# A long-convolution kernel on one core: odd-block chunk sums as three split products, and the chunk sums issued behind half of the Toeplitz products

## The chip, the core and the metric

The kernel runs on one core of a Trainium2 chip. The metric is device time in microseconds (us) of one execution; lower is better. Five engines with their own in-order instruction streams take part: PE (matrix products), ACT, DVE and POOL (elementwise work) and SP (which here only starts DMAs). They meet through semaphores alone.

## The reference, cut to what matters

```python
P = dtA[:, :, None] * jnp.arange(length)            # H=128 channels, N=64 states, L=2048
K = 2.0 * jnp.einsum('hn,hnl->hl', Cs, jnp.exp(P)).real
u_m = x * mask                                       # 64 sequences x 128 channels x 2048
y = irfft(rfft(u_m, 4096) * rfft(K, 4096))[..., :2048]   # a causal convolution per channel
return x + (y + u_m * D[:, None]) * mask
```

All data are float32. Each channel has its own convolution kernel K, built from 64 complex exponentials.

## The kernel before, in words

The kernel computes the convolution without a transform. A sequence of 2048 is cut in 8 chunks of 256, and each chunk in an even and an odd block of 128. Inside a chunk the convolution is a Toeplitz product; between chunks 64 complex states (128 rows) carry the past. After a prologue that builds tables, one **slot** per channel runs 128 times: slots of the first 6 channels and of the last 8 are written out, the 114 between are a hardware loop over groups of 6 channels (`groups`, L215 to L224, with register channel numbers).

A product in float32 costs the PE several passes. Where precision allows, an operand is split into a rounded high part (type fp32r, written by ACT as a copy) and a low part (operand minus high part, written by DVE or POOL), and `three` (L828) issues three fp32r products: high times high, high times low, low times high.

In slot h the PE works for three channels: `here` = h, `one` = h+1, `two` = h+2. Its order before: `chunk_sums(one)`, which forms the new state contributions of the 8 chunks in PSUM bank `v` (three split products for the even blocks, L844, one float32 product for the odd blocks, L847); `turn_x(two)`, 8 transposes of x to PSUM banks `xt_even` and `xt_odd`; `toep_even/toep_odd(here)` for two of the four 128-column pieces; `turn_e(two)`, two transposes; the other two Toeplitz pieces; `from_state(here)`, 12 split products that add the states' part to `y`.

Between `chunk_sums` and `from_state` of a channel stands a scan over its 8 chunks, which goes to and fro between ACT and DVE on bank `v`. Its steps for channel h+1, with the names used below:

1. `turn_odds(h+1)` on ACT (two 64-row copies, in the trace `room<-v 64x192`), after the chunk sums.
2. `pairs(h+1)` on DVE (two dependent operations, `mid` and `v`, 128x192).
3. `turn_pairs(h+1)` on ACT (two copies, 64x128).
4. `fours(h+1)` on DVE (four operations, each dependent on the one before, 128x128 and 128x64). The last one releases `s_evens`; its end is called **E(h+1)** below.
5. `turn_evens(h+1)` on ACT (two copies, 64x192), at the head of ACT's next slot.
6. `odds(h+1)` on DVE (two dependent operations, 128x192), behind `choose(h)`, the two COPY_PREDICATED that merge the finished channel h.
7. `z_high(h+1)` on ACT and then `z_low(h+1)` on DVE: the split states, which `from_state(h+1)` reads.

Order of the other engines in slot h, before. ACT: turn_evens(h), f_high(h+1), turn_odds(h+1), t_high(h+1), z_high(h), x_high(h+2), e_high and e_odd(h+2), turn_pairs(h+1), x_odd(h+2). DVE: choose(h-1), odds(h), pairs(h+1), z_low(h), x_low(h+2), e_low(h+2), fours(h+1). POOL: two broadcast multiplications `tw1`, `tw2` (L421, L422) and their difference `pf` (L428), with `f_low` (L404) and `t_low` (L409) between and behind. SP: load_x(h+3), then, once the PE is through with the Toeplitz products of h, load_t(h+2), then store(h-1).

Of the kernel before, what the change touches and what calls it, by code (L numbers as in the profile page):

```python
# [48 lines left out]
def s4d_kernel(nc, x, length, log_dt, C, log_A_real, A_imag, D, out):  # L49
    ctx = ExitStack()  # L50
    with ctx:
# [52 lines left out]
        zhi = [sb(f"zhi{i}", [P, NC * B], F32R) for i in range(2)]  # L104
        zlo = [sb(f"zlo{i}", [P, NC * B], F32R) for i in range(2)]

        ehi = [sb(f"ehi{i}", [P, P], F32R) for i in range(2)]
        elo = [sb(f"elo{i}", [P, P], F32R) for i in range(2)]
        eod = [sb(f"eod{i}", [P, P]) for i in range(2)]

        tw1, tw2 = (room[:, i].rearrange("p (a b c) -> p a b c", a=2, b=SQ) for i in (5, 6))
        pf = [sb("pf0", [P, 2, CHUNK]), room[:, 7].rearrange("p (a q) -> p a q", a=2)]
# [88 lines left out]
        s_zlo = sem("s_zlo")  # L201
        s_ehi = sem("s_ehi")
        s_elo = sem("s_elo")
        s_eod = sem("s_eod")
        s_fhi = sem("s_fhi")
        s_flo = sem("s_flo")
        s_thi = sem("s_thi")
# [138 lines left out]
        @block.gpsimd  # L346
        def _(pool):
            done = [0]

            def link(ins):  # L350
                done[0] += 1
                ins.then_inc(s_gp, 1)
                pool.wait_ge(s_gp, done[0])


            link(pool.memset(zpad[:], 0.0))
            link(pool.memset(ident[:], 0.0))
            link(pool.affine_select(out=ident[:], in_=ident[:], compare_op=ALU.not_equal, fill=1.0, base=0,
                                    pattern=[[-1, P]], channel_multiplier=1))
            link(pool.iota(mask[0:B, :], pattern=[[2 * CHUNK, CPH], [1, CHUNK]], base=0, channel_multiplier=0))  # L360
            link(pool.iota(mask[B:P, :], pattern=[[2 * CHUNK, CPH], [1, CHUNK]], base=CHUNK, channel_multiplier=0))
            pool.engine_nop().then_inc(s_pool0, 1)


            pool.wait_ge(s_ex0, 1)
            pool.wait_ge(s_ca, 16 * 2)
            c_re = cin[:].rearrange("p (n c) -> p c n", c=2)[:, 0, :]
            c_im = cin[:].rearrange("p (n c) -> p c n", c=2)[:, 1, :]
            pool.tensor_tensor(t1, ar, ar, ALU.mult)
            link(pool.tensor_tensor(t2, ai, ai, ALU.mult))  # L370
            pool.tensor_tensor(norm, t1, t2, ALU.add).then_inc(s_norm, 1)
            link(pool.tensor_tensor(t3, c_im, ai, ALU.mult))
            link(pool.tensor_tensor(g_re, c_re, ar, ALU.mult))
            link(pool.tensor_tensor(g_re, t3, g_re, ALU.subtract))
            link(pool.tensor_tensor(t3, c_im, ar, ALU.mult))
            link(pool.tensor_tensor(g_im, c_re, ai, ALU.mult))
            link(pool.tensor_tensor(g_im, g_im, t3, ALU.add))
            pool.wait_ge(s_norm, 2)
            pool.tensor_tensor(g_re, g_re, norm, ALU.mult).then_inc(s_g, 1)
            pool.tensor_tensor(g_im, g_im, norm, ALU.mult).then_inc(s_g, 1)  # L380

            pool.memset(NB[:, SQ - 1, 1, :], 1.0)
            link(pool.memset(NB[:, SQ - 1, 2, :], 0.0))
            pool.wait_ge(s_lam, 1)
            room_x = W1[:, 0].rearrange("p h i -> p (h i)")
            temps = [room_x[:, q * SQ // 2 * N:(q + 1) * SQ // 2 * N] for q in range(4)]
            link(level(pool, link, NB, 1, 2, 0, temps, 0))
            link(level(pool, link, NB, 1, 2, 0, temps, 1))
            level(pool, link, NB, 1, 2, 0, temps, 2).then_inc(s_nb, 1)
            pool.wait_ge(s_nb, 1)  # L390
            level(pool, link, NB, 1, 2, 0, temps, 3).then_inc(s_nb, 1)

            pool.wait_ge(s_nx, 1)
            part = SQ // 2 * (N - XSPLIT)
            temps = [wide[:, a:a + part] for a in (0, part, 2 * npn, 2 * npn + part)]
            level(pool, link, NX, 0, 1, A_POW, temps, 3, XSPLIT, N).then_inc(s_nxp, 1)
            for t in range(T_R - BANKS, T_R):
                pool.wait_ge(s_free[t % BANKS], t // BANKS + 1)

            def f_low(g, j):  # L400
                pool.wait_ge(s_fhi, chan(g, j) + 1)
                if exists(g, j, -2):
                    pool.wait_ge(s_y, 2 * chan(g, j) - 2)
                pool.tensor_tensor(flo[j % 2][:], pf[j % 2][:, 1, ::-1], fhi[j % 2][:].bitcast(F32),  # L404
                                   ALU.subtract).then_inc(s_flo, 1)

            def t_low(g, j):
                pool.wait_ge(s_thi, chan(g, j) + 1)
                pool.tensor_tensor(tlo[j % 2][:], traw[j % 2][:, ::-1], thi[j % 2][:].bitcast(F32),  # L409
                                   ALU.subtract).then_inc(s_tlo, 1)  # L410

            def channel(g, j):

                h, k = chan(g, j), j % 2
                w1 = W1[:, :, h].unsqueeze(3).broadcast_to([P, 2, SQ, SQ])
                w2 = W2[:, :, h].unsqueeze(3).broadcast_to([P, 2, SQ, SQ])
                b1 = B1[:, h].unsqueeze(1).unsqueeze(1).broadcast_to([P, 2, SQ, SQ])
                b2 = B2[:, h].unsqueeze(1).unsqueeze(1).broadcast_to([P, 2, SQ, SQ])
                if exists(g, j, -1):
                    pool.wait_ge(s_pf, h)  # L420
                pool.tensor_tensor(tw1[:], w1, b1, ALU.mult).then_inc(s_gpa, 1)  # L421
                pool.tensor_tensor(tw2[:], w2, b2, ALU.mult).then_inc(s_gpa, 1)  # L422
                if exists(g, j, -2):
                    f_low(*on(g, j, -2))
                    pool.wait_ge(s_et, h - 1)
                    pool.wait_ge(s_flo, h - 1)
                pool.wait_ge(s_gpa, 2 * h + 2)
                pool.tensor_tensor(pf[k][:], tw1[:].rearrange("p a b c -> p a (b c)"),  # L428
                                   tw2[:].rearrange("p a b c -> p a (b c)"), ALU.subtract).then_inc(s_pf, 1)
                if exists(g, j, -2):  # L430
                    t_low(*on(g, j, -2))

            groups(pool, channel)
            for h in (H - 2, H - 1):
                f_low(h // SLOTS, h % SLOTS)
                t_low(h // SLOTS, h % SLOTS)

        @block.scalar
        def _(act):
# [7 lines left out]
            def x_odd(g, j):  # L447
                act.wait_ge(s_tr, 2 * chan(g, j) + 2)
                copy(uod[j % 3][:], xt[1][:]).then_inc(s_uod, 1)

            act.wait_ge(s_arg, 1)
            for k in range(1, len(POWERS[::2])):
# [37 lines left out]

            def e_high(g, j):
                act.wait_ge(s_et, chan(g, j) + 1)
                copy(ehi[j % 2][:], e_bank(j)[:, 0:P]).then_inc(s_ehi, 1)

            def e_odd(g, j):
                copy(eod[j % 2][:], e_bank(j)[:, P:2 * P]).then_inc(s_eod, 1)

            def f_high(g, j):
                act.wait_ge(s_pf, chan(g, j) + 1)
# [29 lines left out]
            def slot(g, j):  # L529
# [3 lines left out]
                    turn_evens(*here)  # L533
                if has1:
                    f_high(*one)
                    turn_odds(*one)
                    t_high(*one)
                if has0:
                    z_high(*here)
                if has2:  # L540
                    x_high(*two)
                    e_high(*two)
                    e_odd(*two)
                if has1:
                    turn_pairs(*one)
                if has2:
                    x_odd(*two)

            e_high(0, 0)
            e_odd(0, 0)  # L550
            slot(-1, SLOTS - 1)
            groups(act, slot)

# [1 line left out]
        def _(dve):  # L555
# [168 lines left out]
            link(dve.tensor_scalar(mask[:], mask[:], flen[:, 0:1], None, ALU.is_lt))  # L724

            def e_low(g, j):
                dve.wait_ge(s_eod, chan(g, j) + 1)
                less(elo[j % 2][:], e_bank(j)[:, 0:P], ehi[j % 2][:]).then_inc(s_elo, 1)

            def choose(g, j, part):  # L730

# [41 lines left out]
            def slot(g, j):  # L773
# [7 lines left out]
                    choose(*back, 1)  # L781
                if has0:
                    odds(*here)
                if has1:
                    pairs(*one)
                if has0:
                    z_low(*here)
                if has2:
                    x_low(*two)
                    e_low(*two)  # L790
                if has1:
                    fours(*one)
# [11 lines left out]
        def _(pe):  # L804
# [7 lines left out]
            def turn_x(g, j, par):  # L812
                pe.wait_ge(s_x[j], 32 * (g + 1))
                if exists(g, j, -1):
                    pe.wait_ge(s_uod if par else s_ulo, chan(g, j))
                for c in range(CPH):
                    b = 2 * c + par
                    mm = pe.transpose(xt[par][:, c * P:(c + 1) * P], xs[j][:, b * BLK:(b + 1) * BLK], ident[:])  # L818
# [15 lines left out]
            def chunk_sums(g, j):  # L834
# [6 lines left out]
                pe.wait_ge(s_ulo, h + 1)  # L841
                if exists(g, j, -2):
                    pe.wait_ge(s_zlo, h - 1)
                three(v, ehi[k][:], elo[k][:], uhi[j % 3][:, cols], ulo[j % 3][:, cols], True, False)  # L844
                pe.wait_ge(s_eod, h + 1)
                pe.wait_ge(s_uod, h + 1)
                pe.matmul(v, eod[k][:], uod[j % 3][:, cols], start=False, stop=True,  # L847
                          skip_group_check=True).then_inc(s_in, 1)

            def y_cols(g, j, c):  # L850
                return yb[j % 2][c // 2][:, (c % 2) * CHUNK:(c % 2 + 1) * CHUNK]
# [28 lines left out]
            def slot(g, j):  # L880

                here, one, two = (g, j), on(g, j, 1), on(g, j, 2)
                has0, has1, has2 = exists(g, j, 0), exists(g, j, 1), exists(g, j, 2)
                if has1:
                    chunk_sums(*one)
                if has2:
                    turn_x(*two, 0)
                    turn_x(*two, 1)
                if has0:
                    for c in range(2):  # L890
                        toep_even(*here, c)
                        toep_odd(*here, c)
                if has2:
                    turn_e(*two)
                if has0:
# [90 lines left out]
```

## Time and profile before

| | us |
|---|---|
| median of 3 runs | 881.8 (881.62 to 883.14) |
| the profiled execution | 882.78 |
| its span, first to last instruction | 880.9 |
| PE busy in the span | 828.1 (94%) |
| DVE, POOL, ACT busy | 755.0, 636.9, 624.6 |

The profiled execution is 1.0 us over the median, and 1.9 us of it lie outside the span. The first 76 us are the prologue; the slots fill the rest. In a timeline a row is start, duration, engine, line, operation and its tiles; what stands in square brackets is idle time of the engine just before, and what ended it. All activations of the loop carry L441, since a helper issues them: they are told apart by their tiles and shapes.

### The profile page before, as it was taken

The page shows a single profiled execution, that of the slowest core. Times are in us where ns is not written, and L with a number is a line of the kernel's source. Part 1 is how long each engine was busy: PE and PEld are TensorE (multiplying, and loading weights), DVE is VectorE, ACT ScalarE, POOL GpSimd, SP SyncE. Part 2 cuts the span into 40 slices and gives each one's busy share as a digit, 9 for nine tenths or more (in the row PEclk, how much of TensorE's full clock was granted, in tenths as well). Part 3 has the DMA queues.
Part 4 walks back from the last instruction along what each step waited for, and adds up shares of the span by engine and source line. Part 5 has one row for each costly group of instructions (what it writes and reads, how often), then busy time and mean ns, then how long its engine had stood idle before and what let it go on. Part 6 is the DMA issues. An engine that isn't in the chain of part 4 may idle for free.

```text
span 880.9 us, 22605 instructions
## 1 busy us (share of the span) xinstructions
PE 828.1 (94%) x6218; PEld 760.6 (86%) x6218; DVE 755.0 (86%) x2054; ACT 624.6 (71%) x1710; POOL 636.9 (72%) x692
## 2 busy tenths in 40 slices
PE   0377999999999999999999999999999999999997
PEld 0366988999988999999999999999999999999996
DVE  8976988888888888888888888888888888888886
ACT  2095767776767777777777777777777777777774
POOL 3727877777777877777787777777777778777771
PEclk9789999999999999999999999999999999999999
DMA  3002677777777777777777777777777777777775
GB/s 83 0 1 49 175 177 191 186 196 177 192 179 188 189 191 186 197 185 196 185 196 187 190 192 186 196 185 195 187 195 189 189 190 188 192 189 197 190 197 132
DMA packets 160947, 151.66 MB, mean 172 GB/s; under 512 B 13216, under 2 KB 160928, under 8 KB 160928
## 3 DMA queue, kind: packets, MB, share of 16 engines
q1 hardware_dynamic: 160928, 151.43, 67.8%
q8 instruction: 9, 0.15, 0.1%
q14 instruction: 10, 0.08, 0.0%
HBM read 84.08 MB, written 67.30 MB: 172 GB/s over the span
## 4 chain that ended last, share of the span: by engine, by line
PE 83%; DVE 5%; DMA 5%; ACT 2%; SPq 2%; POOL 1%; issue 1%; POOLq 0%; DVEq 0%
PE y L830 13%; PE y L832 13%; PE y L831 12%; PE y L865 12%; PE v L847 10%; PE xt_even L818 6%; PE xt_odd L818 6%; DMA xall<-in_x_dram 5%; PE v L830 3%; PE v L831 3%; PE v L832 3%; PE y L825 1%; PE y L826 1%; SPq L301 1%; ACT W L441 1%
## 5 line engine op out<-in xcount | busy, mean ns | idle before, releaser
L441 ACT ACTIVATE room<-v 64x192 f32<-64x192 f32 (+1 forms) x768 | 235.8, 307 | 173.6 <-DVE v L738 157.1
L738 DVE SCALAR_TENSOR_TENSOR v<-v,RV,mid 128x192 f32<-128x192 f32 (+2 forms) x512 | 192.4, 376 | 57.2 <-DVE mid L738 2.7
L738 DVE SCALAR_TENSOR_TENSOR mid<-room,RV,v 128x192 f32<-128x192 f32 (+2 forms) x512 | 184.2, 360 | 41.7 <-ACT room L441 22.2
L830 PE MATMUL y<-thi,uhi 128*128 128x256 f32 x512 | 186.4, 364 | 0.2 <-POOL tlo L409 0.2
L734 DVE COPY_PREDICATED xall<-mask,y 128x512 f32<-128x512 int32 x256 | 176.0, 736 | 1.4 <-issue 1.4
L830 PE MATMUL y<-fhi,zhi 128*128 128x256 f32 x512 | 154.6, 302 | 0.8 <-DVE zlo L564 0.7
L421 POOL TENSOR_TENSOR room<-W,B 128x512 f32 (+1 forms) x128 | 135.8, 1061 | 13.7 <-DVE W L708 13.6
L832 PE MATMUL y<-thi,ulo 128*128 128x256 f32 x512 | 144.5, 282 | 0.0
L832 PE MATMUL y<-fhi,zlo 128*128 128x256 f32 x512 | 144.0, 281 | 0.0
L831 PE MATMUL y<-tlo,uhi 128*128 128x256 f32 x512 | 144.0, 281 | 0.0
L831 PE MATMUL y<-flo,zhi 128*128 128x256 f32 x512 | 144.0, 281 | 0.0
L422 POOL TENSOR_TENSOR room<-W,B 128x512 f32 (+1 forms) x128 | 135.7, 1060 | 0.0
L865 PE MATMUL y<-traw,uod 128*128 128x128 f32 x680 | 130.5, 273 | 0.0
L818 PEld LDWEIGHTS xt_even<-ident,xall 128*128 128x128 f32 x512 | 63.7, 142 | 68.2 <-issue 56.5
L404 POOL TENSOR_TENSOR flo<-pf,fhi 128x256 fp32r<-128x256 f32 x64 | 46.8, 731 | 83.9 <-ACT fhi L441 83.9
L865 PEld LDWEIGHTS y<-traw,uod 128*128 128x128 f32 x680 | 104.8, 189 | 0.0
L404 POOL TENSOR_TENSOR flo<-room,fhi 128x256 fp32r<-128x256 f32 x64 | 46.7, 730 | 76.6 <-ACT fhi L441 76.6
L831 PEld LDWEIGHTS y<-tlo,uhi 128*128 128x128 f32 x512 | 98.3, 192 | 0.2 <-issue 0.2
L830 PEld LDWEIGHTS y<-thi,uhi 128*128 128x128 f32 x512 | 97.5, 191 | 0.7 <-POOL tlo L409 0.5
L830 PEld LDWEIGHTS y<-fhi,zhi 128*128 128x128 f32 x512 | 96.7, 189 | 1.2 <-issue 1.1
L831 PEld LDWEIGHTS y<-flo,zhi 128*128 128x128 f32 x512 | 96.9, 189 | 0.0
L832 PEld LDWEIGHTS y<-fhi,zlo 128*128 128x128 f32 x512 | 96.7, 189 | 0.0
(174 smaller groups left out, 1981.0 us busy)
## 6 DMA issues: line engine op xcount, KB each, us to landing
xall<-in_x_dram SPq DMA_DIRECT2D x256, 256.0 KB, 4.6
out_dram<-xall SPq DMA_DIRECT2D x254, 256.0 KB, 3.4
traw<-krows SPq DMA_DIRECT2D x128, 128.0 KB, 3.0
out_dram<-xall SPq DMA_DIRECT2D x4, 128.0 KB, 2.4
krows<-ksb SPq DMA_DIRECT2D x8, 16.0 KB, 1.8
cin<-in_L_cond_C_dram SPq DMA_DIRECT2D x1, 64.0 KB, 2.0
dall<-in_L_cond_D_dram SPq DMA_DIRECT2D x1, 64.0 KB, 2.4
krows<-zpad SPq DMA_DIRECT2D x1, 63.5 KB, 6.3
```

The costliest lines, as they stand in the source:

```text
L404: pool.tensor_tensor(flo[j % 2][:], pf[j % 2][:, 1, ::-1], fhi[j % 2][:].bitcast(F32), ALU.subtract).then_inc(s_flo, 1)
L421: pool.tensor_tensor(tw1[:], w1, b1, ALU.mult).then_inc(s_gpa, 1)
L422: pool.tensor_tensor(tw2[:], w2, b2, ALU.mult).then_inc(s_gpa, 1)
L441: return act.activation(dst, src, ACT.Copy)
L734: dve.copy_predicated(xs[j][:, a:a + 512], mask[:, a:a + 512], yb[j % 2][part][:]).then_inc(s_pred, 1)
L738: return dve.scalar_tensor_tensor(out=out, in0=src, scalar=RV[:, h, k:k + 1], in1=other, op0=ALU.mult, op1=ALU.add)
L818: mm = pe.transpose(xt[par][:, c * P:(c + 1) * P], xs[j][:, b * BLK:(b + 1) * BLK], ident[:])
L830: pe.matmul(o, a_hi, b_hi, start=start, stop=False, skip_group_check=True)
L831: pe.matmul(o, a_hi, b_lo, start=False, stop=False, skip_group_check=True)
L832: return pe.matmul(o, a_lo, b_hi, start=False, stop=stop, skip_group_check=True)
L847: pe.matmul(v, eod[k][:], uod[j % 3][:, cols], start=False, stop=True, skip_group_check=True).then_inc(s_in, 1)
L865: mm = pe.matmul(y_cols(g, j, c)[:, BLK:2 * BLK], uod[j % 3][:, b], traw[k][:, :BLK - 1:-1], start=False, stop=False, skip_group_check=True)
```

## The change

The odd block's transposed x gets a split as the even block's has: `oddhi` (ACT, a second copy of `xt_odd` behind the one to `uod`) and `oddlo` (POOL, `uod - oddhi`). `ehi` and `elo` are widened from 128 to 256 columns, so that one ACT copy and one DVE subtraction cover both halves of the transposed table; the separate float32 copy `eod` goes. The float32 product of the chunk sums becomes three fp32r products.

The PE's `chunk_sums(one)` moves from the head of the slot to behind the first two Toeplitz pieces. The orders of ACT and DVE change too: on ACT turn_odds(h+1) now stands behind z_high(h), and x_odd (two copies) and e_high stand between turn_odds and turn_pairs; on DVE pairs(h+1) now stands behind x_low and z_low.

```diff
 # POOL
+            def odd_low(g, j):
+                pool.wait_ge(s_oddhi, chan(g, j) + 1)
+                pool.tensor_tensor(oddlo[j % 2][:], uod[j % 3][:], oddhi[j % 2][:].bitcast(F32),
+                                   ALU.subtract).then_inc(s_oddlo, 1)
...
                 pool.tensor_tensor(tw1[:], w1, b1, ALU.mult).then_inc(s_gpa, 1)
+                if exists(g, j, -3):
+                    odd_low(*on(g, j, -2))
                 pool.tensor_tensor(tw2[:], w2, b2, ALU.mult).then_inc(s_gpa, 1)
...
+            odd_low(0, 0)
             groups(pool, channel)
 # ACT
                 copy(uod[j % 3][:], xt[1][:]).then_inc(s_uod, 1)
+                copy(oddhi[j % 2][:], xt[1][:]).then_inc(s_oddhi, 1)
...
-                copy(ehi[j % 2][:], e_bank(j)[:, 0:P]).then_inc(s_ehi, 1)
-
-            def e_odd(g, j):
-                copy(eod[j % 2][:], e_bank(j)[:, P:2 * P]).then_inc(s_eod, 1)
+                copy(ehi[j % 2][:], e_bank(j)).then_inc(s_ehi, 1)
...
                     turn_evens(*here)
                 if has1:
                     f_high(*one)
-                    turn_odds(*one)
+                if has2:
+                    x_high(*two)
+                if has1:
                     t_high(*one)
                 if has0:
                     z_high(*here)
+                if has1:
+                    turn_odds(*one)
                 if has2:
-                    x_high(*two)
+                    x_odd(*two)
                     e_high(*two)
-                    e_odd(*two)
                 if has1:
                     turn_pairs(*one)
-                if has2:
-                    x_odd(*two)
 # DVE
-                dve.wait_ge(s_eod, chan(g, j) + 1)
-                less(elo[j % 2][:], e_bank(j)[:, 0:P], ehi[j % 2][:]).then_inc(s_elo, 1)
+                dve.wait_ge(s_ehi, chan(g, j) + 1)
+                less(elo[j % 2][:], e_bank(j), ehi[j % 2][:]).then_inc(s_elo, 1)
...
                 if has0:
                     odds(*here)
+                if has2:
+                    x_low(*two)
+                if has0:
+                    z_low(*here)
                 if has1:
                     pairs(*one)
-                if has0:
-                    z_low(*here)
                 if has2:
-                    x_low(*two)
                     e_low(*two)
                 if has1:
                     fours(*one)
 # PE
-                    pe.wait_ge(s_uod if par else s_ulo, chan(g, j))
+                    pe.wait_ge(s_oddhi if par else s_ulo, chan(g, j))
...
-                pe.wait_ge(s_eod, h + 1)
-                pe.wait_ge(s_uod, h + 1)
-                pe.matmul(v, eod[k][:], uod[j % 3][:, cols], start=False, stop=True,
-                          skip_group_check=True).then_inc(s_in, 1)
+                pe.wait_ge(s_oddlo, h + 1)
+                three(v, ehi[k][:, P:2 * P], elo[k][:, P:2 * P], oddhi[k][:, cols], oddlo[k][:, cols], False,
+                      True).then_inc(s_in, 1)
...
-                if has1:
-                    chunk_sums(*one)
                 if has2:
                     turn_x(*two, 0)
                     turn_x(*two, 1)
...
                         toep_even(*here, c)
                         toep_odd(*here, c)
+                if has1:
+                    chunk_sums(*one)
                 if has2:
                     turn_e(*two)
```

## Rows read from the trace of the kernel before

**Rows 1.** The page's busy times of the engines over the span.
```profile
PE 828.1 (94%) x6218; PEld 760.6 (86%) x6218; DVE 755.0 (86%) x2054; ACT 624.6 (71%) x1710; POOL 636.9 (72%) x692
```
**Rows 2.** Stretches of the loop, PE: length, busy (instructions), granted clock, DMA share, GB/s.
```profile
400.00:500.00 100.00, 100.00 (x762) 1.00 0.74 190
```
**Rows 3.** Tile v, 300 to 800 us: count, duration min/median/max, first and last start.
```profile
L830 PE MATMUL v<-uhi,ehi x81: 367/367/368, 302.0 to 797.7; 128*128 128x448 f32 x81
```
**Rows 4.** Chain that ended last, 500 to 514 us: start, length, what.
```profile
506.44 0.12 PE y L832
506.56 0.20 PE v L830
...
507.17 0.75 PE v L847 x2
```
**Rows 5.** Who waited for whom, 300 to 800 us: total, times, longest.
```profile
ACT room L441 <- DVE v L738: 102.9, 81, 1.3
```
**Rows 6.** Timeline of DVE, 598 to 613 us: the scan's operations, and z_low.
```profile
599.51 0.29 DVE L738 SCALAR_TENSOR_TENSOR v<-v,RV,mid 128x64 f32<-128x64 f32 x1
...
600.99 0.40 DVE L738 SCALAR_TENSOR_TENSOR mid<-room,RV,v 128x192 f32<-128x192 f32 x1
601.42 0.42 DVE L738 SCALAR_TENSOR_TENSOR v<-v,RV,mid 128x192 f32<-128x192 f32 x1
601.79 0.41 DVE L738 SCALAR_TENSOR_TENSOR mid<-room,RV,v 128x192 f32<-128x192 f32 x1
602.34 0.43 DVE L738 SCALAR_TENSOR_TENSOR v<-v,RV,mid 128x192 f32<-128x192 f32 x1
603.06 0.62 DVE L564 TENSOR_TENSOR zlo<-v,zhi 128x448 fp32r<-128x448 f32 x1 [0.29 <-ACT zhi L441]
...
604.57 0.35 DVE L738 SCALAR_TENSOR_TENSOR mid<-room,RV,v 128x128 f32<-128x128 f32 x1
...
605.99 0.29 DVE L738 SCALAR_TENSOR_TENSOR v<-v,RV,mid 128x64 f32<-128x64 f32 x1
```
**Rows 7.** Timeline of ACT, 598 to 613 us: most of one slot.
```profile
607.00 0.42 ACT L441 ACTIVATE fhi<-room 128x256 fp32r<-128x256 f32 x1
607.44 0.66 ACT L441 ACTIVATE room<-v 64x192 f32<-64x192 f32 x2
...
608.84 0.55 ACT L441 ACTIVATE zhi<-v 128x448 fp32r<-128x448 f32 x1 [0.29 <-DVE v L738]
609.27 0.59 ACT L441 ACTIVATE uhi<-xt_even 128x512 fp32r<-128x512 f32 x1
609.75 0.29 ACT L441 ACTIVATE ehi<-y 128x128 fp32r<-128x128 f32 x1
...
610.23 0.55 ACT L441 ACTIVATE room<-v 64x128 f32<-64x128 f32 x2
```
**Rows 8.** Timeline of DVE, 866 to 881 us: first and last step of the last fours.
```profile
869.53 0.35 DVE L738 SCALAR_TENSOR_TENSOR mid<-room,RV,v 128x128 f32<-128x128 f32 x1
...
870.62 0.29 DVE L738 SCALAR_TENSOR_TENSOR v<-v,RV,mid 128x64 f32<-128x64 f32 x1
```
**Rows 9.** Timeline of POOL, 598 to 613 us: one round without its tw2 and t_low.
```profile
604.00 1.07 POOL L421 TENSOR_TENSOR room<-W,B 128x512 f32 x1
...
607.58 0.73 POOL L404 TENSOR_TENSOR flo<-room,fhi 128x256 fp32r<-128x256 f32 x1 [1.49 <-ACT fhi L441]
608.54 1.28 POOL L428 TENSOR_TENSOR room<-room 128x512 f32<-128x512 f32 x1 [0.23 <-POOL flo L404]
...
610.48 1.06 POOL L421 TENSOR_TENSOR room<-W,B 128x512 f32 x1
```
**Rows 10.** Timeline of SP, 498 to 520 us: load_t and the next load_x.
```profile
505.31 0.35 SPq L308 DMA_DIRECT2D traw<-krows  x1
...
507.62 1.55 SPq L296 DMA_DIRECT2D xall<-in_x_dram  x2
```
**Rows 11.** The page's DMA issues: count, KB each, median us from issue to landing.
```profile
xall<-in_x_dram SPq DMA_DIRECT2D x256, 256.0 KB, 4.6
```

More of the change, by code:

```diff
@@ L105, in s4d_kernel @@
         zlo = [sb(f"zlo{i}", [P, NC * B], F32R) for i in range(2)]
-        ehi = [sb(f"ehi{i}", [P, P], F32R) for i in range(2)]
-        elo = [sb(f"elo{i}", [P, P], F32R) for i in range(2)]
-        eod = [sb(f"eod{i}", [P, P]) for i in range(2)]
+        oddhi = [sb(f"oddhi{i}", [P, NC * B], F32R) for i in range(2)]
+        oddlo = [sb(f"oddlo{i}", [P, NC * B], F32R) for i in range(2)]
+        ehi = [sb(f"ehi{i}", [P, 2 * P], F32R) for i in range(2)]
+        elo = [sb(f"elo{i}", [P, 2 * P], F32R) for i in range(2)]
         tw1, tw2 = (room[:, i].rearrange("p (a b c) -> p a b c", a=2, b=SQ) for i in (5, 6))
@@ L203, in s4d_kernel @@
         s_elo = sem("s_elo")
-        s_eod = sem("s_eod")
+        s_oddhi = sem("s_oddhi")
+        s_oddlo = sem("s_oddlo")
         s_fhi = sem("s_fhi")
@@ L431, in channel @@
                     t_low(*on(g, j, -2))
+            odd_low(0, 0)
             groups(pool, channel)
             for h in (H - 2, H - 1):
+                odd_low(h // SLOTS, h % SLOTS)
                 f_low(h // SLOTS, h % SLOTS)
@@ L539, in slot @@
                     z_high(*here)
+                if has1:
+                    turn_odds(*one)
                 if has2:
-                    x_high(*two)
+                    x_odd(*two)
                     e_high(*two)
-                    e_odd(*two)
                 if has1:
                     turn_pairs(*one)
-                if has2:
-                    x_odd(*two)
             e_high(0, 0)
-            e_odd(0, 0)
             slot(-1, SLOTS - 1)
@@ L843, in chunk_sums @@
                     pe.wait_ge(s_zlo, h - 1)
-                three(v, ehi[k][:], elo[k][:], uhi[j % 3][:, cols], ulo[j % 3][:, cols], True, False)
-                pe.wait_ge(s_eod, h + 1)
-                pe.wait_ge(s_uod, h + 1)
-                pe.matmul(v, eod[k][:], uod[j % 3][:, cols], start=False, stop=True,
-                          skip_group_check=True).then_inc(s_in, 1)
+                three(v, ehi[k][:, 0:P], elo[k][:, 0:P], uhi[j % 3][:, cols], ulo[j % 3][:, cols], True, False)
+                pe.wait_ge(s_oddlo, h + 1)
+                three(v, ehi[k][:, P:2 * P], elo[k][:, P:2 * P], oddhi[k][:, cols], oddlo[k][:, cols], False,
+                      True).then_inc(s_in, 1)
             def y_cols(g, j, c):
```

## The prediction, made before the changed kernel ran

> **What bounds the kernel now.** I read the busy times first: the PE works 94% of the span, DVE 86%, POOL 72%, ACT 71% [rows 1]. Shares alone don't name the bound, so next comes the loop by stretches: in the middle the PE is busy 100 us of 100, at a granted clock of 1.00, that is 2.4 GHz [rows 2]. The slot follows from the first product of the chunk sums: 81 starts from 302.0 to 797.7 us are 80 slots of 495.7/80 = **6.20 us** [rows 3]. The PE is packed, so before the change a slot is the sum of the PE's work. Last I looked at what is next. ACT waits for DVE 81 times in 81 slots, 102.9/81 = 1.27 us each [rows 5]: that is turn_evens(h) waiting for E(h). ACT is not short of time, it is in a chain with DVE, and this chain turns once per slot. It is nearly as long as the slot; the change must be read against it, not against the PE alone.
>
> **The change, part by part.**
>
> *PE.* In the chain the float32 product takes 0.75 us, one fp32r product of the same 448 columns 0.20 to 0.205 (506.56 to 507.17 is three of them) [rows 4]. The slot loses 0.75 and gains 3 x 0.205 = 0.615: -0.135, so 6.06 us if the PE stays packed. The moved products cost no more in their new place.
>
> *POOL.* One round goes from 604.00 to 610.48 = 6.48 us, of which 1.49 is waiting for f_high: 4.99 us of work, the 0.23 us in front of pf counted in [rows 9]. odd_low is new: a subtraction of 512 columns with both inputs and the output in SBUF. The nearest row is pf, the same shape and operation: 1.28 us [rows 9]. Bounds: the cheapest 512-column row, 1.06; twice the 256-column f_low, 1.46. I take 1.28, so POOL needs 4.99 + 1.28 = 6.27 us per slot (6.05 to 6.45). POOL goes from a spare engine to one that needs slightly more than the old slot. odd_low also adds a wait, for oddhi; queued behind it are tw2, f_low, pf and t_low, for which the PE's turn_e and Toeplitz products wait. In the slot worked out below oddhi(h+2) ends at about +4.5, while POOL comes to odd_low(h+2) at about +5.2 (f_low at +1.2, then 610.48 - 607.58 = 2.90 to tw1, and 1.06 for that), so the wait is met. In front of the first channel odd_low stands once alone: 0 to 1.3 us, I take 1.
>
> *ACT.* New are the oddhi copy (as uhi, 0.59) and a wider e_high; e_odd goes [rows 7]. e_high at 256 columns lies between 0.29 (128) and 0.59 (512): by columns 0.39. ACT needs about 0.7 us more work per slot, and has 1.27 us of waiting, so its load is no bound [rows 5]. Its **order** is.
>
> *DVE.* e_low goes from 128 to 256 columns. It adds more than nothing and less than the 0.62 that z_low's 448 columns take in all [rows 6]; it runs while ACT is busy with turn_pairs and isn't on the path below.
>
> *The chain.* All engines issue in order. In the new order one slot contains this closed loop: E(h), choose(h-1), odds(h) on DVE; z_high(h), **then** turn_odds(h+1) on ACT; pairs(h+1) on DVE; turn_pairs(h+1) on ACT; fours(h+1) on DVE, which ends at E(h+1). Before, turn_odds(h+1) stood ahead of z_high(h) and pairs(h+1) directly behind odds(h) (601.42 and 601.79 in rows 6), while z_low, x_low and e_low filled the DVE during turn_pairs. Now turn_odds(h+1) can't start before odds(h) is done, and turn_pairs(h+1) stands behind x_odd, oddhi and e_high. From E(h) = 0, for a slot of the hardware loop:
>
> - choose and odds: E is 599.51 + 0.29 = 599.80; odds starts at 600.99 (+1.19), its second operation at 601.42 and ends 601.84: **+2.04** [rows 6]. Between two dependent operations of this shape I also see 0.55 in place of 0.43 (601.79 to 602.34). I take 0.49: +2.10.
> - hand-over to z_high 0.03: +2.13 (in rows 7 it starts within 0.03 of the end of odds).
> - z_high 0.55. A turned copy doesn't start before the copy in front of it has ended: 607.00 + 0.42 = 607.42, start at 607.44 [rows 7]. So z_high 0.55, turn_odds 0.66, each with 0.02 to 0.03 behind it: 1.24.
> - x_odd and oddhi: two copies of 512 columns from PSUM follow each other at 0.48 (609.27 to 609.75) to 0.54; I take 0.51 each, 1.02. e_high 0.39 + 0.02.
> - turn_pairs 0.55. It ends at 2.13 + 1.24 + 1.02 + 0.41 + 0.55 = **+5.35**. pairs doesn't delay it: its first operation can start 0.15 behind turn_odds, and 0.55 + 0.43 later it ends, at about +4.5; ACT comes to turn_pairs at +4.80.
> - hand-over to DVE: 0.03 to 0.20 by the gaps of these rows (dependent operations leave 0.14 between end and start, 601.79 + 0.41 to 602.34); I take 0.14.
> - fours from 604.57 to 605.99 + 0.29 = 1.71 [rows 6].
>
> E(h+1) is at 5.35 + 0.14 + 1.71 = **7.20 us**, 1.00 us over the old slot. In the written-out slots DVE's hand-overs are shorter: the last fours takes 869.53 to 870.91 = 1.38 [rows 8]. With 0.04 in front of it and odds ending at +2.04 that is 5.29 + 0.04 + 1.38 = **6.71 us**.
>
> In such a slot the PE has 7.20 - 6.06 = 1.1 us to spare. z_low(h) starts 0.03 to 0.15 behind z_high and takes 0.62 [rows 6], so from_state(h) can start at about +3.5. From there to the end of the chunk sums of h+2 the PE does less than one whole slot, so they end before 3.5 + 6.06 = 9.6; turn_odds(h+2) comes to its turn on ACT at 7.20 + 2.13 + 0.57 = 9.9. So the later place of the chunk sums doesn't itself set the slot. POOL's 6.27 fits in 7.20, and what hides odd_low is POOL's waiting.
>
> *SP and DMAs.* turn_x now opens the PE's slot, 1.36 us (the old chunk sums) earlier. load_x is issued 507.62 - 505.31 = 2.3 us behind load_t, which follows the Toeplitz products [rows 10], and lands 4.6 us later [rows 11], about 7.2 us behind those products. With 6.06 us slots it is needed one from_state (12 products of 0.12 [rows 4] = 1.44) and one slot behind them, 7.5 us: 0.3 us of margin. With 7.20 us slots the margin is over 1 us: no cost.
>
> *Weighed against a rule.* The four dependent steps of fours take 1.71 us in the loop and 1.38 in the written-out end [rows 6, 8]. The Trainium skill (VectorE: DVE Perf Modes, The DRAIN you can't avoid) says that a semaphore behind each of a row of Vector operations costs nothing extra. The written-out end agrees with it, the loop's rows don't; by that rule every slot would be as the last one, 6.71 us and not 7.20, and the time that of the second case below.
>
> **Sum.** 114 loop slots x 1.00 = 114 us; 12 written-out slots x (6.71 - 6.20) = 6; start 1. Together +121 on the profiled execution's 882.8 = 1004; this execution is 1 us over the median, so against 881.8 I predict **1003 us**. With the larger value of every row (odds to 2.16, copies at 0.54, hand-over 0.20) a loop slot is 7.20 + 0.06 + 0.06 + 0.06 = 7.38: 881.8 + 114 x 1.18 + 7 = 1023, with 0.02 more on a slot **1025**.
>
> **The rivals.**
>
> 1. *Same chain, short hand-overs everywhere*: 6.71 us, 126 x 0.51 + 1 = 65 us, **947**. For it: rows 8. Against it: the loop's own rows, the 1.71 of fours above all.
> 2. *POOL bounds.* If the chain closed in less than POOL's 6.27 us, the slot would be 6.27: +0.07 x 126 = 9, **891** (880 to 913 by the bounds of odd_low). For it: the row of pf. Against: the chain, whose bare durations alone, with ACT's copies overlapped as densely as any row shows (0.43, 0.66, 0.48, 0.48, 0.39 - 0.11 = 0.28, 0.55 = 2.88 [rows 7]), are 1.19 + 0.82 + 2.88 + 1.29 (rows 8 without three gaps of 0.03) = 6.18 before any hand-over. The Trainium skill (GPSIMD Engine Reference, Engine selection) advises VectorE for elementwise work, as about twice as fast on two inputs; the price here is a row's.
> 3. *PE bounds, faster.* The place is the PE's slot: -0.135 x 126 = -17, **865**. It decides if chain, POOL and load_x all fit in 6.06 us. POOL would need odd_low at 1.06 or less, and the chain no hand-over time and shorter copies than any row. Against it stands the 6.18 above.
> 4. *The split moves nothing*, because the slot is set by something that both kernels have: within 2 us of **882**. Nothing in the rows speaks for it.
>
> **How the numbers follow.** The chain at 7.20 has 0.82, case 1 0.08, case 2 0.04, case 3 0.03, case 4 0.03. The forecast is the likeliest. Its own range is 947 to 1025, which contains cases of partly short hand-overs; the range given, 942 to 1025, adds a little for copies that overlap more, and leaves out cases 2 to 4 and the far tails. A measurement here can tell about 0.2% (1.8 us) from no change. Faster: case 3 and a share of case 2, 0.04; same: case 4, 0.03; slower: the rest, 0.93.
>
> **What would show it.** In the trace of after: starts of the first chunk-sum product 7.2 us apart; the PE idle about 1.1 us per slot, in front of from_state's first product, released by DVE's zlo; ACT waiting for E about 1.9 us per slot (7.20 - 5.35) in place of 1.27; a new DVE wait for ehi in front of e_low; turn_pairs directly behind e_high on ACT, with pairs long done; odd_low near 1.28 us; POOL still waiting for fhi, about 0.9 us. Wrong would be a packed PE, a POOL without idle time, or turn_odds waiting for the PE.

## The result, and the profile after

| | before | after |
|---|---|---|
| median (runs) | 882.5 us (881.6 to 883.2) | 1009.1 us (1007.9 to 1009.6) |
| span of the profiled execution | 880.9 us | 1007.3 us |
| loop slot, from the first chunk-sum product | 6.20 us | 7.23 us |

The changed kernel is slower by a factor of 1.143 (95% interval 1.141 to 1.145). Predicted were 1003 us, range 942 to 1025.

The page's busy times, and the shares of the chain that ended last by engine, with those of the kernel before in the last line:

```profile
PE 867.2 (86%) x6346; PEld 787.0 (78%) x6346; DVE 803.7 (80%) x2054; ACT 666.2 (66%) x1710; POOL 794.2 (79%) x820
...
ACT 35%; DVE 32%; issue 26%; DVEq 3%; POOL 1%; PE 1%; ACTq 1%; DMA 0%; SPq 0%; POOLq 0%
...
PE 83%; DVE 5%; DMA 5%; ACT 2%; SPq 2%; POOL 1%; issue 1%; POOLq 0%; DVEq 0%
```

Where rows 1 show the PE at 94%, no engine is now above 86%. The PE carried 83% of the chain before; now it has 1% of it, and ACT and DVE share it, with "issue", time in which an engine waited for nothing that the profile shows. That is the picture of a bound by waiting: everybody is idle some of the time. Who waited for whom, 300 to 800 us (total, times, longest), the answer to rows 5:

```profile
ACT room L452 <- DVE v L747: 132.5, 70, 1.9
POOL flo L406 <- ACT fhi L452: 71.1, 69, 1.4
...
PEld y L835 <- DVE xall L743: 40.1, 69, 0.9
PE y L840 <- DVE zlo L573: 34.7, 69, 0.6
DVE mid L747 <- ACT room L452: 31.4, 138, 0.3
DVE elo L573 <- ACT ehi L452: 19.2, 69, 0.3
```

Each of these happens once or twice in each of the 69 slots. ACT's wait for E grew from 1.27 us [rows 5] to 132.5/70 = 1.89. POOL waits 71.1/69 = 1.03 us per slot, so it isn't the bound although odd_low is new. The PE waits twice: for the merged x in front of turn_e (PEld is its weight load) and for zlo in front of from_state.

One slot in which nothing else happens, first DVE (start, duration), the answer to rows 6:

```profile
618.23 1.38 DVE L743 COPY_PREDICATED xall<-mask,y 128x512 f32<-128x512 int32 x2
...
619.51 0.40 DVE L747 SCALAR_TENSOR_TENSOR mid<-room,RV,v 128x192 f32<-128x192 f32 x1
619.94 0.42 DVE L747 SCALAR_TENSOR_TENSOR v<-v,RV,mid 128x192 f32<-128x192 f32 x1
620.27 0.68 DVE L573 TENSOR_TENSOR ulo<-xt_even,uhi 128x512 fp32r<-128x512 f32 x1
620.97 0.62 DVE L573 TENSOR_TENSOR zlo<-v,zhi 128x448 fp32r<-128x448 f32 x1
621.79 0.41 DVE L747 SCALAR_TENSOR_TENSOR mid<-room,RV,v 128x192 f32<-128x192 f32 x1 [0.19 <-ACT room L452]
622.34 0.43 DVE L747 SCALAR_TENSOR_TENSOR v<-v,RV,mid 128x192 f32<-128x192 f32 x1
623.04 0.42 DVE L573 TENSOR_TENSOR elo<-y,ehi 128x256 fp32r<-128x256 f32 x1 [0.28 <-ACT ehi L452]
623.73 0.35 DVE L747 SCALAR_TENSOR_TENSOR mid<-room,RV,v 128x128 f32<-128x128 f32 x1 [0.27 <-ACT room L452]
...
625.15 0.29 DVE L747 SCALAR_TENSOR_TENSOR v<-v,RV,mid 128x64 f32<-128x64 f32 x1
```

and ACT in the same slot, the answer to rows 7:

```profile
618.35 0.66 ACT L452 ACTIVATE room<-v 64x192 f32<-64x192 f32 x2 [1.89 <-DVE v L747]
...
620.40 0.54 ACT L452 ACTIVATE zhi<-v 128x448 fp32r<-128x448 f32 x1 [0.16 <-DVE v L747]
620.97 0.66 ACT L452 ACTIVATE room<-v 64x192 f32<-64x192 f32 x2
621.65 0.60 ACT L452 ACTIVATE room<-xt_odd 128x512 f32<-128x512 f32 x1
622.14 0.59 ACT L452 ACTIVATE oddhi<-xt_odd 128x512 fp32r<-128x512 f32 x1
622.62 0.39 ACT L452 ACTIVATE ehi<-y 128x256 fp32r<-128x256 f32 x1
623.04 0.55 ACT L452 ACTIVATE room<-v 64x128 f32<-64x128 f32 x2
625.48 0.66 ACT L452 ACTIVATE room<-v 64x192 f32<-64x192 f32 x2 [1.89 <-DVE v L747]
```

In these rows the loop through E can be followed step by step: odds ends at 620.36 on DVE, z_high starts at 620.40 on ACT; turn_odds, x_odd, oddhi, e_high and turn_pairs follow without a gap until 623.59; fours starts at 623.73 and ends at 625.44; ACT's next turn_evens, at 625.48, has waited 1.89 us for that. pairs was done at 622.77, and turn_pairs came only at 623.04, behind e_high.

### The profile page after: what moved, and what is told of

The parts are those of the page before. It is cut to its first block, busy times and chain, and to the rows that moved or that the text cites. A ratio compares the mean times of both kernels' runs of the same rounds, so it can differ in the third digit from the quotient of the medians.

```text
span 1007.3 us, 22842 instructions
## 1 busy us (share of the span) xinstructions
PE 867.2 (86%) x6346; PEld 787.0 (78%) x6346; DVE 803.7 (80%) x2054; ACT 666.2 (66%) x1710; POOL 794.2 (79%) x820
## 4 chain that ended last, share of the span: by engine, by line
ACT 35%; DVE 32%; issue 26%; DVEq 3%; POOL 1%; PE 1%; ACTq 1%; DMA 0%; SPq 0%; POOLq 0%
ACT room L452 18%; DVE mid L747 13%; DVE v L747 12%; ACT oddhi L452 6%; ACT uod L452 5%; ACT ehi L452 3%; DVEq L747 3%; DVE xall L743 3%; ACT zhi L452 1%; ACT W L452 1%; DVE q L600 0%; ACTq L504 0%; ACT bsel L452 0%; ACT B L452 0%; POOL room L431 0%
## 5 line engine op out<-in xcount | busy, mean ns | idle before, releaser
L416 POOL TENSOR_TENSOR oddlo<-uod,oddhi 128x512 fp32r<-128x512 f32 x85 | 109.0, 1282 | 14.7 <-DVE W L717 14.2
L842 PEld LDWEIGHTS y<-thi,ulo 128*128 128x128 f32 x512 | 96.3, 188 | 0.0
```

Of the source, the lines that this page charges most:

```text
L416: pool.tensor_tensor(oddlo[j % 2][:], uod[j % 3][:], oddhi[j % 2][:].bitcast(F32), ALU.subtract).then_inc(s_oddlo, 1)
L842: return pe.matmul(o, a_lo, b_hi, start=False, stop=stop, skip_group_check=True)
```

## The experiments

Time is the median of each run, and its ratio is to the kernel before measured beside it on the same chip (879.9 to 884.1 us); a slot is the distance of the first chunk-sum products of a run between 300 and 800 us.

**The orders alone.** The split is left out, PE, ACT and DVE issue in the new order. To the kernel before (ACT shown, DVE and PE as in the change):

```diff
-                    turn_odds(*one)
+                if has2:
+                    x_high(*two)
...
+                    turn_odds(*one)
                 if has2:
+                    x_odd(*two)
                     e_high(*two)
                     e_odd(*two)
                 if has1:
                     turn_pairs(*one)
```

> The orders alone: PE, ACT and DVE issue in the new order, but the odd block keeps its one float32 product, so there is no oddhi, no odd_low, and e_high and e_odd are two copies of 128 columns. Theory: turn_odds(h+1) behind z_high(h) keeps the loop long; without the oddhi copy ACT is through with x_odd, e_high and e_odd at about +4.4, and turn_pairs waits for pairs (+4.5) instead of +4.80: slot 7.23 - 0.27 = 6.96, about 972 us (955 to 985). Rival A (the split costs the time): within 5 us of before's 882. Rival B (late chunk sums): over 955 too, with turn_odds waiting for the PE.

Measured: 977.3 us, ratio 1.110 (1.109 to 1.112), slot 6.98. Most of the loss is there without oddhi, odd_low or the three products, so rival A falls. The slot has the expected length, since turn_pairs now waits 0.21 us for DVE in place of standing behind oddhi:

```profile
625.98 0.55 ACT L441 ACTIVATE room<-v 64x128 f32<-64x128 f32 x2 [0.21 <-DVE v L740]
```

Between 300 and 800 us ACT waits for nothing but DVE here, never for the PE: the sign of rival B, turn_odds waiting for late chunk sums, is absent. This run moves PE, ACT and DVE together; ACT's and DVE's new order with the PE's old one was not run.

**The low half left out.** odd_low goes, and the product that used the low half takes the high half.

```diff
-                if exists(g, j, -3):
-                    odd_low(*on(g, j, -2))
...
-                three(v, ehi[k][:, P:2 * P], elo[k][:, P:2 * P], oddhi[k][:, cols], oddlo[k][:, cols], False,
+                three(v, ehi[k][:, P:2 * P], elo[k][:, P:2 * P], oddhi[k][:, cols], oddhi[k][:, cols], False,
                       True).then_inc(s_in, 1)
```

> The changed kernel without odd_low: POOL doesn't make the low half, and the product that used it takes the high half in its place, so part of the sum is computed from other data; everything else, the orders too, is as in the changed kernel. POOL has 1.28 us per slot less to do. Theory: POOL was waiting for f_high anyway, the time stays at 1009 us (1003 to 1012), and POOL's wait for fhi grows from about 1.0 to 2.3 us per slot. Rival A (odd_low, by its time on POOL or by disturbing DVE's memory accesses): at least 20 us less.

Measured: 1007.8 us, ratio 1.145 (1.143 to 1.147), slot 7.23 as in the changed kernel. 1.28 us of POOL work per slot are worth nothing here; POOL waits for them instead:

```profile
POOL flo L406 <- ACT fhi L448: 158.6, 70, 2.7
```

That is 158.6/70 = 2.27 us per slot. Rival A falls.

**Only e_high between turn_odds and turn_pairs.**

```diff
                 if has2:
-                    x_odd(*two)
                     e_high(*two)
                 if has1:
                     turn_pairs(*one)
+                if has2:
+                    x_odd(*two)
```

> The changed kernel with x_odd (both copies of xt_odd) behind turn_pairs on ACT, so only e_high stands between turn_odds and turn_pairs. Theory: turn_pairs no longer waits for ACT's queue but for pairs on DVE, about 0.24 us earlier in the slot; slot 6.98, 1009 - 126 x 0.24 = 979 us (974 to 990), and oddhi ends later but is still in time for odd_low. Rival (what stands between turn_odds and turn_pairs is covered by other waits): within 5 us of 1009. Second rival (oddhi that late holds up odd_low and the chunk sums, as in the run with the split alone): over 1009.

Measured: 983.5 us, ratio 1.113 (1.110 to 1.116), slot 7.01. Two copies that stood in ACT's queue, and that nobody on the path needed, cost 0.22 us per slot by their place alone. One part of the expectation failed: oddhi is no longer in time for odd_low. POOL waits 57.1/72 = 0.79 us per slot for it, and the PE 45.6/72 = 0.63 us in front of the transposes to xt_odd, but neither wait lies on the loop through E.

**All slots written out.**

```diff
-            with eng.Fori(1, GROUPS - 1) as g:
+            for g in range(1, GROUPS - 1):
                 for j in range(SLOTS):
                     body(g, j)
```

> The changed kernel with its 114 loop slots written out too: no hardware loop, no register channel numbers; the same instructions in the same order. Theory (the chain through E sets the slot, and the loop lengthens its hand-overs): every slot is as the written-out ones at the end of the changed kernel's trace, 6.71 us in place of 7.23, so 1009 - 114 x 0.52 = 950 us (942 to 958). Rival (the slot is set by engine work or waits that don't depend on hand-overs, POOL or PE): within 8 us of 1009.

Measured: 951.4 us, ratio 1.076 (1.073 to 1.079), slot 6.72. The steps of fours, 622 us into this run, on DVE (start, duration):

```profile
622.55 0.35 DVE L747 SCALAR_TENSOR_TENSOR mid<-room,RV,v 128x128 f32<-128x128 f32 x1 [0.15 <-ACT room L452]
622.93 0.36 DVE L747 SCALAR_TENSOR_TENSOR v<-v,RV,mid 128x128 f32<-128x128 f32 x1
623.33 0.28 DVE L747 SCALAR_TENSOR_TENSOR mid<-room,RV,v 128x64 f32<-128x64 f32 x1
623.64 0.29 DVE L747 SCALAR_TENSOR_TENSOR v<-v,RV,mid 128x64 f32<-128x64 f32 x1
```

They take 1.38 us, 1.71 in the loop. That is 0.33 of the 0.51 us by which the slot is shorter; 0.11 more lies between the end of turn_pairs and fours (0.03 in place of 0.14), and 0.08 is the turn of the loop, 0.46 once in six slots. So a part of the slot is hand-overs, and they are longer in the hardware loop, but not all: the second step of odds starts 0.04 us behind the first in the loop too (median of 69 slots), where those of pairs and fours start 0.14 behind. Which property of the loop lengthens them (the waits on register values, the register-addressed operand RV or another) was not separated, and odds, which has both, shows that these two alone don't do it.

**The control: before, written out.** The same diff to the kernel before.

> The kernel before with its 114 loop slots written out, nothing else. It is the control to the versions above: theory: PE bounds before with 6.20 us per slot and the hand-overs of DVE lie beside it, so the time stays within 3 us of before (879 to 885 where before has 882). Rival (writing out is itself what gains): under 875.

Measured: 880.6 us, ratio 1.0005 (0.9995 to 1.0015). The same shorter hand-overs bring nothing where the PE sets the slot, and 58 us where the loop through E does.

**The split alone.** The changed kernel with the orders of before on PE, ACT and DVE.

> The split alone: oddhi, oddlo, the wide ehi and elo and the three products stay, but PE, ACT and DVE issue in the order of before. Theory (the order on ACT and DVE makes the slot long): the loop through E closes in about 6.1 us again, PE needs 6.06, and POOL with 6.27 us is the last: slot 6.27, about 891 us (880 to 900), POOL nearly without waits. Rival A (the split itself, odd_low on POOL or the two extra ACT copies, costs the time): 950 us or more. Rival B (the late chunk sums cost the time): under 882, since they are early again.

Measured: 943.5 us, ratio 1.073 (1.071 to 1.074), slot 6.66. None of the expectations held: the loop through E is short again, but another one has closed. Waits between 300 and 800 us (total, times, longest), then one round on ACT and one on POOL (start, duration):

```profile
PEld v L837 <- POOL oddlo L416: 53.0, 75, 0.7
POOL oddlo L416 <- ACT oddhi L452: 33.6, 76, 0.5
ACT room L452 <- PE v L839: 33.5, 75, 0.5
```

```profile
601.23 0.66 ACT L452 ACTIVATE room<-v 64x192 f32<-64x192 f32 x2 [0.45 <-PE v L839]
...
604.96 0.59 ACT L452 ACTIVATE oddhi<-xt_odd 128x512 fp32r<-128x512 f32 x1
```

```profile
605.63 1.29 POOL L416 TENSOR_TENSOR oddlo<-room,oddhi 128x512 fp32r<-128x512 f32 x1 [0.45 <-ACT oddhi L452]
...
612.31 1.28 POOL L416 TENSOR_TENSOR oddlo<-uod,oddhi 128x512 fp32r<-128x512 f32 x1 [0.46 <-ACT oddhi L452]
```

odd_low starts 0.08 us behind oddhi, the PE's odd products start behind odd_low, turn_odds behind the products, and oddhi stands last in ACT's slot. 605.63 to 612.31 is one slot, 6.68.

**The same with oddlo's product last.** This tests that loop: two products of 0.2 us leave it.

```diff
-                pe.wait_ge(s_oddlo, h + 1)
-                three(v, ehi[k][:, P:2 * P], elo[k][:, P:2 * P], oddhi[k][:, cols], oddlo[k][:, cols], False,
-                      True).then_inc(s_in, 1)
+                pe.wait_ge(s_oddhi, h + 1)
+                pe.matmul(v, ehi[k][:, P:2 * P], oddhi[k][:, cols], ...)
+                pe.matmul(v, elo[k][:, P:2 * P], oddhi[k][:, cols], ...)
+                pe.wait_ge(s_oddlo, h + 1)
+                pe.matmul(v, ehi[k][:, P:2 * P], oddlo[k][:, cols], ..., stop=True).then_inc(s_in, 1)
```

> The split alone in the order of before, as in the run that gave 943 us, with one change: the product with oddlo is the last of the six, and only it waits for odd_low. Theory for the 943 us: a loop odd_low(h+1), odd products on PE, ACT's whole slot from turn_odds to oddhi, odd_low(h+2), 6.67 us long. Two products of 0.2 us leave this loop: 6.26, and POOL's 6.27 is the next bound; about 893 us (885 to 905). Rival (POOL's load or disturbed DVE accesses made the 943 us): no change, 938 or more.

Measured: 899.3 us, ratio 1.017 (1.015 to 1.020), slot 6.28. The order of three products is worth 44 us, and the slot is now POOL's 6.27: POOL's waits come to 0.2 us per slot, the 0.23 in front of pf that the 6.27 contains.

**The PE's move alone.** The changed kernel with ACT's and DVE's order of before.

> The split and PE's new order (chunk sums behind two Toeplitz pieces), but ACT and DVE issue in the order of before. Theory: turn_odds(h+1) comes to its turn early and now waits for the PE; a loop over two slots goes z_low(h), from_state(h), turn_x, two Toeplitz pieces, chunk sums of h+2 (4.8 us from z_low's end to s_in), scan of h+2 up to z_low (about 7.7 us or more): 12.5/2 = 6.26 us or somewhat more, so a slot of 6.3 to 6.6, 895 to 935 us, with ACT waiting for PE v in front of turn_odds. Rival B (the later chunk sums are what costs the time): 990 us or more. Rival A (the split): 950 or more with POOL busy throughout.

Measured: 1038.7 us, ratio 1.181 (1.179 to 1.183), slot 7.44: slower than the change itself, and the expected length was wrong.

```profile
ACT room L452 <- PE v L839: 95.1, 67, 1.4
...
PE y L837 <- DVE zlo L571: 76.0, 67, 1.1
```

I had looked for a loop over two slots and missed one over a single slot. In the old order z_high(h) stands behind turn_odds(h+1) on ACT, and that waits for the late chunk sums of h+1; so from_state(h) on the PE waits by way of ACT and DVE for products that the PE itself has issued just before, and the chunk sums of h+2 come behind it. The new order on ACT and DVE is therefore what the PE's move needs: it exchanges a loop of 7.44 us for one of 7.2.

**Taking the found waits away.** The split in the order of before, all slots written out, with the late oddlo product, oddhi and e_high behind turn_pairs on ACT, and e_low behind fours on DVE.

> A version that takes away each wait found so far: the split in the order of before, all slots written out, products ordered by when their operands come (oddlo last), on ACT uod ahead of turn_pairs and oddhi and e_high behind it, on DVE e_low behind fours. Theory: the loops over E (about 5.9 us) and over oddhi and odd_low close in time, and what is left is PE with 6.06 and POOL with 6.10 to 6.27 us: 866 to 891 us. Rival (the split can't pay here since odd_low always comes too late for the PE): 895 us or more.

Measured: 882.7 us, ratio 0.999 (0.997 to 1.0005): no difference to the kernel before that can be told. Starts of the chunk sums were 6.09 us apart in the median, 6.18 on average. The waits that are left come now and then, for load_x and load_t:

```profile
PEld xt_even L830 <- DMA xall<-in_x_dram: 6.5, 11, 1.1
ACT thi L452 <- DMA traw<-krows: 6.4, 13, 1.0
```

The kernel before waits here too, but less: 2.7 us for load_x and 1.2 for load_t in the same 500 us. The prediction's margin of 0.3 us for load_x doesn't explain it, for that was worked out with turn_x at the head of the PE's slot, and here the chunk sums stand there again; but load_x took 5.2 us to land in place of 4.6. That these waits are what holds the slot at 6.18 is argued, not shown. Three tries to give the load more room by SP's order made it far worse:

> The version before this one, with SP's order changed: store(h-1) first, then load_x, one channel further ahead (h+4), and load_t last. There, starts of the chunk sums were 6.18 us apart, but 6.11 where no load came late: PE waited 17 times in 81 slots for a load of x, up to 1.1 us. Theory: the loads are the last wait on PE's way; without it the slot is POOL's 6.10: 882 - 126 x 0.08 = 872 us (866 to 877), under before's time. Rival (the waits for loads take the place of others, or the DMAs as a whole are the bound): 879 or more.

> As the version that gave 883 us, but SP issues load_t first as it did there, then load_x one channel further ahead (h+4), and the store last. The version with the store first gave 972 us, where load_t, behind 512 KB of other transfers, landed 4.8 us after its issue in place of 3.1, and ACT's t_high waited for it in front of z_high in nearly every slot. Theory: with load_t first again and load_x 1.3 us earlier, neither is waited for: slot 6.10 to 6.12 us, 870 to 877 us. Rival (the DMAs as a whole bound it): 880 or more.

> As the run beside it, with t_high behind z_high on ACT, so that a late load_t holds up POOL's t_low at most and not the states. Theory: what was left of waits for traw in front of z_high (6.4 us in 500 in the version that gave 883 us) goes; 869 to 876 us, at most 5 us less than the run beside it. Rival (t_low's later start stops POOL, which has no slack): more than the run beside it.

Measured: 971.9, 967.3 and 964.8 us, ratios 1.103, 1.096 and 1.092. In the first, load_t landed 4.8 us behind its issue in place of 3.1, and ACT waited for it in front of z_high. In the second and third this was to be mended, but load_t landed no sooner (4.9 and 5.1 us). With the store last, only one load_t stands between it and the load_x that has to wait for it to land, as load_x(h+4) reuses the buffer that store(h-2) empties. Of the second:

```profile
SPq L298 <- DMA out_dram<-xall: 358.0, 122, 5.0
```

That is 2.9 us per slot in which SP's queue stands still, and the next store and load_t behind it. It closes a loop of its own, and between 600 and 614 us the chain consists of it alone: a store lands 4.4 to 5.2 us after its issue, then load_x and the next store are issued, 6.4 to 6.7 us in all. So the third says nothing on t_high by itself. load_x(h+3) between load_t and the store was not tried. A version that beats the kernel before was not found.

## Why the prediction was right, point by point

The loop through E was the bound, as forecast, and its terms can be set against the slot shown above (E = 618.31 before it, the end of the fours before):

| term | predicted | measured |
|---|---|---|
| E to the end of odds | 2.10 | 620.36 - 618.31 = 2.05 |
| to z_high's start | 0.03 | 0.04 |
| z_high and turn_odds | 1.24 | 621.65 - 620.40 = 1.25 |
| x_odd and oddhi | 1.02 | 622.62 - 621.65 = 0.97 |
| e_high | 0.41 | 0.42 |
| turn_pairs | 0.55 | 0.55 |
| hand-over, fours | 0.14 + 1.71 | 0.14 + 1.71 |
| slot | 7.20 | 625.44 - 618.31 = 7.13 |

Five slots of each group of six have 7.13 to 7.20, the one at the turn of the hardware loop 7.60; the mean is 7.23. This turn wasn't in the sum. In the kernel before it costs nothing: the distance of two E is 6.38 there at the turn and 6.01 in the slot behind it, since the PE sets the pace. 114 slots from E(6) to E(120) take 711.1 us before and 823.8 us after, +112.8 where 114 were forecast. That this came out so close is partly luck: the plain slots are 0.05 us shorter than the sum, the turn adds 0.46/6 = 0.08, and the 114 slots of before have 6.24 us on average and not the 6.20 of 300 to 800 us. The written-out slots run at 6.71 us exactly as worked out.

Mis-sized was the rest: +7 were forecast for start and written-out slots, 13.6 came. 5.1 of them lie at the end, 8.5 at the start. Of these, 2.6 are the forecast 0.5 for each of five written-out slots; the other 5.9 lie ahead of E(1), where I counted odd_low alone, at 1 us. The moved chunk sums of channel 1 stand there behind the first Toeplitz pieces, which need POOL's first t_low. PE, with its idle time, and then PE's stretches (length, busy, granted clock):

```profile
84.95 0.39 PE L840 MATMUL y<-thi,uhi 128*128 128x256 f32 x1 [2.88 <-POOL tlo L411]
...
87.25 0.57 PE L842 MATMUL v<-uhi,elo 128*128 128x448 f32 x1
87.62 0.57 PE L840 MATMUL v<-oddhi,ehi 128*128 128x448 f32 x1
```

```profile
85.00:88.00 3.00, 3.00 (x15) 0.65 0.00 0
```

The PE stood still for 2.9 us, then the granted clock was 0.65 on average in this stretch, and a product took 0.37 us in place of 0.205; before, the same stretch had 1.00. The second slot took 9.47 us in place of 5.57. odd_low isn't what makes it long: without it the second slot takes 10.22 us, with the orders alone 10.33, and with the split alone 9.03. The granted clock fell to 0.50 there too, in stretches between 76 and 88 us. How much of the 5.9 us is the order and how much the clock was not separated.

PE: three products cost 0.615 us, as taken, but where the PE isn't the bound this is worth nothing. Its waits are 1.1 us per slot as forecast, but not all in front of from_state: 40.1/69 = 0.6 us stand in front of turn_e, which waits for choose, and 34.7/69 = 0.5 in front of from_state. The wait at turn_e changes no time, since e_high comes later still. (By busy time the PE is idle 0.7 us per slot; the ends of products are modelled.) POOL: odd_low 1.28 us, as pf; its wait for f_high is 1.03 (0.9 forecast). ACT's wait for E is 1.89 (1.9 forecast), and turn_odds never waits for the PE between 300 and 800 us.

The rivals: short hand-overs everywhere were tested by writing the slots out, 951 us where the rival's number was 947. The gaps between the four steps of fours are 0.03 to 0.04 us there, and 0.14 to 0.15 in the hardware loop, 0.33 us over the four. The Trainium skill (VectorE: DVE Perf Modes, The DRAIN you can't avoid) measured, on a row of copies, that a semaphore behind each Vector operation costs nothing extra. The written-out trace agrees with that as far as it goes, for no run here leaves the semaphores out; the loop's trace differs, and the measurement decides. POOL was no bound of this kernel, but became it when the loops through E and through oddhi were opened (6.28 us); the waits for loads came up last, at 6.18.

Not foreseen was what each half does alone. The prediction treated the split as harmless but for POOL's 6.27 us, and in the old order it costs 64 us (943.5 against 879.9) by a loop through oddhi and oddlo; and it said that the late chunk sums don't set the slot, which holds in the changed kernel, but with ACT's and DVE's old order they make the slot 7.44.

## What to carry to other kernels

Where several engines work in order on a software pipeline, write down for a change of order each closed loop that goes once round a slot, from an operation to the same operation for the next channel, and sum durations, hand-overs and whatever stands in between in each queue; the longest loop is the slot, and no engine needs to be busy. Look for loops over one slot on every pair of engines before those over two. An engine with idle time still lengthens such a loop by each copy that stands ahead of the one that is waited for, and a product whose operand comes last is to be issued last.

## What the hardware showed that I had not expected

- In the hardware loop the dependent DVE steps of pairs and fours start 0.14 us behind the end of the one before, written out 0.03 to 0.04; the step of odds, which follows choose, starts 0.04 behind in both. With the turn of the loop that is 7.23 against 6.72 us per slot, 58 us for this kernel, and nothing for the kernel before.
- The turn of the hardware loop costs the slot it falls in 0.46 us (7.60 against 7.14), and nothing over a group of six where the PE sets the slot.
- A 64-row ACT copy of this kernel, which moves rows between partition halves, starts only when the copy in front of it has ended (0.02 to 0.03 behind it), and the copy behind it as late; copies of 128 rows overlap by 0.1 us (0.59 long, 0.48 apart). Whether the move or the number of rows does it was not separated.
- At the start of the changed kernel the PE had no work for 2.9 us. When it resumed, at 84.95 us, the granted clock was 0.99 (1.00 before the gap); from 85.9 to 89.2 us it was 0.50 (1.2 GHz), then 1.00 again.
